# Splitting the four final loads of routed results between the queues of SyncE and ScalarE

## What is computed

```python
x = x + tanh(g_xattn[0]) * xattn(layernorm(x), ctx, ctx, mask, Wq, Wk, Wv, Wo, 16)   # 16 heads of 64
x = x + tanh(g_ffn[0]) * ffn(layernorm(x), ...)

# ffn, for h = layernorm(x), t = 1024 tokens
shared = (silu(h @ shared_gate.T) * (h @ shared_up.T)) @ shared_down.T
probs = sigmoid(h @ router_w.T + routing_bias)
scores, idx = top_k(probs, 2)                  # of 8 experts
scores = scores / scores.sum(-1)
combined = sum over the two chosen e of  w[t, e] * (silu(h @ gate_w[e]) * (h @ up_w[e])) @ down_w[e]
return shared + combined
```

## Time and profile before

| | us |
|---|---|
| executions | 178.86, 178.73, 178.04 |
| median | 178.73 |
| span of the profiled execution, first to last instruction | 177.0 |
| TensorE busy (matmul) in the span | 163.7 (93%) |
| VectorE / ScalarE / GpSimd busy | 127.1 / 109.9 / 110.7 |
| mean granted TensorE clock | 0.990 of full speed |

### The profile page before, as it was taken

The page is one execution under the profiler, slowest core; times in us unless marked ns, Lnnn a source line. Parts: engine busy times, 40 slices in busy tenths (PEclk is TensorE's granted clock), DMA queues, the critical chain, the costliest instruction groups (busy, mean ns, idle before and its releaser), DMA issues.

```text
span 177.0 us, 4529 instructions
## 1 busy us (share of the span) xinstructions
PE 163.7 (93%) x1412; PEld 139.0 (79%) x1412; DVE 127.1 (72%) x612; ACT 109.9 (62%) x404; POOL 110.7 (63%) x139
## 2 busy tenths in 40 slices
PE   7999889999999999999999999988899999998970
PEld 7777669997879998779998787986587878776860
DVE  2879988755898676888676979877857676665273
ACT  4567997558697447787646968744546666655300
POOL 3775799846786835868624768687644466656611
PEclk9999999999999999999999999999999999999996
DMA  5899995810000000000000000012222222220272
GB/s 151 280 373 378 414 403 206 352 62 0 19 2 4 15 2 4 30 21 15 30 4 0 15 21 15 17 50 54 85 76 66 74 63 67 63 77 31 57 233 90
DMA packets 11094, 17.33 MB, mean 98 GB/s; under 512 B 2075, under 2 KB 6945, under 8 KB 10944
## 3 DMA queue, kind: packets, MB, share of 16 engines
q1 hardware_dynamic: 9504, 14.59, 24.0%
q0 software_dynamic: 1280, 2.20, 3.8%
q10 hardware_dynamic: 288, 0.26, 0.4%
HBM read 9.99 MB, written 7.51 MB: 99 GB/s over the span
## 4 chain that ended last, share of the span: by engine, by line
PE 54%; DVE 12%; ACT 10%; POOL 9%; DMA 6%; issue 6%; SPq 1%; DVEq 0%; POOLq 0%
PE misc L408 8%; PE s_even L371 6%; PE o_bank L397 6%; ACT probs L722 4%; PE pt L382 4%; PE proj_q L328 4%; PE pt L658 3%; DMA ys<-probsT,xg 3%; PE proj_k L328 3%; DVE probs L931 3%; PE misc L482 3%; PE proj_q L329 2%; PE proj_q L330 2%; PE proj_k L330 2%; POOL ys L1436 2%
## 5 line engine op out<-in xcount | busy, mean ns | idle before, releaser
L722 ACT ACTIVATE probs<-probs,negmax 128x128 f32<-128x128 f32 x128 | 50.0, 394 | 8.5 <-DVE negmax L931 8.5
L1327 POOL TENSOR_TENSOR probs<-probs,rinv 128x512 f32<-128x512 f32 x32 | 33.1, 1048 | 24.4 <-DVE rinv L945 24.3
L1436 POOL DMA_INDIRECT ys<-probsT,xg x23 | 22.6, 982 | 17.1 <-issue 10.1
L722 ACT ACTIVATION_READ_ACCUMULATOR probs<-probs,negmax 128x1 f32 x128 | 24.3, 190 | 0.0
L931 DVE CUSTOM_DVE_ANT_0 probs<-s_even,mask 128x128 f32<-128x128 f32 x64 | 18.1, 283 | 3.8 <-issue 3.8
L1357 POOL DMA_INDIRECT xs<-xrow,slot x16 | 16.3, 1020 | 6.8 <-issue 3.9
L382 PE MATMUL pt<-ident_sb,probs 128*128 128x128 f32 x128 | 17.6, 277 | 1.6 <-POOL probs L1327 1.0
L371 PE MATMUL s_odd<-kT,qT 64*128 64x128 f32 x128 | 18.5, 285 | 0.0
L371 PE MATMUL s_even<-kT,qT 64*128 64x128 f32 x128 | 18.5, 284 | 0.0
L931 DVE CUSTOM_DVE_ANT_0 probs<-s_odd,mask 128x128 f32<-128x128 f32 x64 | 18.1, 283 | 0.0
L658 PEld LDWEIGHTS pt<-down_sb,v 128*128 128x128 f32 x92 | 12.1, 190 | 7.6 <-issue 7.5
(11 more groups left out here) (282 smaller groups left out, 458.8 us busy)
## 6 DMA issues: line engine op xcount, KB each, us to landing
xs<-pad SPq DMA_DIRECT2D x5, 858.0 KB, 6.3
xg<-xs SPq DMA_DIRECT2D x23, 66.0 KB, 1.9
down_sb<-down SPq DMA_DIRECT2D x1, 1152.0 KB, 9.6
probs<-ys SPq DMA_DIRECT2D x4, 256.0 KB, 4.0
gu_raw<-gu SPq DMA_DIRECT2D x3, 256.0 KB, 5.8
wk_raw<-wkT SPq DMA_DIRECT2D x2, 256.0 KB, 3.6
wq_raw<-wqT SPq DMA_DIRECT2D x2, 256.0 KB, 4.8
mask<-mask SPq DMA_DIRECT2D x8, 64.0 KB, 1.9
```

What stands on the lines that cost most here:

```text
L722: e = act.activation(probs[:, r, l, :], probs[:, r, l, :], ACT.Exp, bias=negmax[:, r, l:l + 1], scale=-1.0, accum_out=rowsum[:, r, l:l + 1])
L1327: pool.tensor_tensor(quad, quad, rinv[:, r, 4 * u:4 * u + 4].unsqueeze(2).to_broadcast([P, 4, P]), ALU.mult).then_inc(norm_done, 1)
L1436: pool.indirect_dma_start(out=ys, out_offset=bass.IndirectOffsetOnAxis(ap=xg[n % IN_FLIGHT][:, P:P + 1].bitcast(U32), axis=0), in_=y_sb[n ...
```

## The change

SyncE raises a new semaphore `y_landed` when its waits for the scatters are over, and issues loads 0 and 2 only. ScalarE waits for that semaphore after its last `block_y` and issues loads 1 and 3, ahead of `silu(2)`, `silu(3)` and its stores.

```diff
@@ semaphores
-        out_sem = sem("out_sem")
+        out_sem, y_landed = sem("out_sem"), sem("y_landed")
@@ SyncE, after `for i in range(IN_FLIGHT): sp.wait_ge(y_out[i], due[i])`
-            for n in range(4):
+            sp.sem_inc(y_landed, 1)
+            for n in (0, 2):
                 load_y(sp, n)
             store_out(sp, 0)
             store_out(sp, 2)
@@ ScalarE
             block_y(BLOCKS - 1)
+            act.wait_ge(y_landed, 1)
+            for n in (1, 3):
+                load_y(act, n)
             for unit in range(2, 4):
                 silu(unit)
             store_out(act, 1)
```

## The result

The change is slower: 179.58 us (median of 22 executions, 178.34 to 180.11) against 178.85 us for the kernel before (22 executions in the same comparison), a ratio of 1.0031 with a 95% interval of 1.0018 to 1.0045, or +0.55 us (0.3 to 0.8); the two medians lie 0.73 us apart, inside the same interval. The forecast of 178.5 us had the wrong sign, and 179.58 lies just outside the range, which ended at 179.5.

The account below looks back on a forecast made before the run. VectorE's unbroken run and the loads through GpSimd were taken as level, with GpSimd's drain ending the program. VectorE's +0.43 and an earlier GpSimd drain gave a 176.70 span (-0.27); with 1.76 added, 178.5 us, range 177.8 to 179.5.

Parts of the forecast that it names:

- the landings: Loads 2 and 3 on two queues: taken to land at 170.9 and 171.2, bounds 1.0 us earlier and unchanged.
- 1 us of slack: Load 0 at VectorE's first addition: landed at 169.3, over 1 us before it was wanted at 170.39.
- The room I saw: DMA engines between 168.5 and 169.0: only 115 GB/s moved while the second issue's packets were late, against 377 later.
- The rival "nothing": Both queues feed the same engines and loads 2 and 3 land as before: 178.7 us, chance 0.20.
- ScalarE's wait and issues: ScalarE before silu(2): wait costs 0.13 us, two issues put silu(2) at 167.17, covered by its 0.78 us idle.
- the long value: A load issue of 1.06 us falling to ScalarE: silu(2) starts at 167.80, VectorE's run begins 0.19 us late.
- GpSimd's drain: End of program: drain counts from GpSimd's last addition, 3.36 us after it, so it would end at 175.96.
- The port: SBUF: VectorE's two-input additions and GpSimd's pair additions exclude each other, costing VectorE 0.43 us in the kernel before.
- My +0.43: VectorE's run: two delays of 0.43 from earlier pair additions, less the present 0.43; bounds -0.43 and +1.0.
- The sum: Whole program: SyncE's drain last, span 176.70 against 177.0, or -0.27 us, giving 178.5 us.
- 0.76: Chance given to a time that can't be told from no change, within 0.5% or 0.89 us.
- my slower case: ScalarE held by its issues past 167.8, so silu(3), hidden(3) and add_shared(0) start late: middle 179.4 us, chance 0.20.

Follow-up runs that it names:

- wait_only: The kernel before, with SyncE raising y_landed and ScalarE waiting for it, all four loads still issued by SyncE: ratio 1.0002 (0.9966 to 1.0038).
- pool_pad: The kernel before, with one more GpSimd addition (128x128, result unused) behind its two pair additions: ratio 1.0020 (0.9998 to 1.0041).
- no_pool: The kernel before, with both pair additions moved from GpSimd to VectorE: ratio 0.9985 (0.9968 to 1.0003).
- change_again: The change itself, measured once more against the kernel before: ratio 1.0015 (0.9990 to 1.0041).
- halves: The change, with SyncE issuing loads 0 and 1 and ScalarE loads 2 and 3: ratio 1.0028 (1.0003 to 1.0053) to the kernel before.
- no_tail: The kernel before, without GpSimd's scatters of blocks 21 and 22, which hold no row for these inputs: ratio 1.0010 (0.9988 to 1.0031).
- hold: The change, with all four loads back on SyncE and ScalarE issuing two tiny loads (1 KB in all) instead: ratio 1.0031 (1.0008 to 1.0053) to the kernel before.
- hold_again: All four loads on SyncE, two tiny loads issued by ScalarE, measured a second time against the kernel before: ratio 1.0024 (1.0000 to 1.0048).
- after_pool_one: The change, with GpSimd's second pair addition moved to VectorE: ratio 0.9995 (0.9977 to 1.0013) to the kernel before.
- act_late: The change, with ScalarE issuing loads 1 and 3 after silu(2) and silu(3): ratio 1.0023 (1.0000 to 1.0046) to the kernel before.
- hold_act: All four loads on SyncE; ScalarE waits for y_landed, then makes five 128x64 copies in place of its two issues: ratio 1.0005 (0.9979 to 1.0032) to the kernel before.

## Why the prediction was wrong

**The step that failed** is that of the landings: "With the durations of before they would land at 170.6 and 170.8 ... Bounds: 1.0 us earlier, and unchanged." I carried times to landing measured with one queue over to two, and gave no bound on the late side. For load 0 I wrote "That instruction also delays load 0 by 0.07, against 1 us of slack: nothing", and counted only the issue. Measured: load 0 took 4.85 us instead of 3.09, 0.7 more than its slack; load 2 landed at 6.08 instead of 5.42. The room I saw, the dip to 115 GB/s, was there and was filled (0.50 MB in the first 3.0 us instead of 0.35), but it did not move the last landing: load 3 came at 6.25, before at 6.07. What was moved earlier was of two loads at once, so neither was complete earlier, and the rate then fell to 238 GB/s where it had been 314 and more.

**The rival "nothing"** came nearest, and I cited it for the wrong thing. The section of the Trainium skill's page DMA: Bandwidth & Descriptors on issuing engines that are not separate queues says that the transfers run on the same engines and interleave. By that rule the trace agrees, 0.25 and 0.25 MB in the first 3.0 us, and landings at 4.85 and 5.04 us. I took from it only that a gain may fail to come. The same trace shows more: SyncE's queue moved 0.10 MB less than before in that time, and load 0 was late by it.

**ScalarE's wait and issues.** The wait cost nothing that shows, as said (wait_only 1.0002, 0.9966 to 1.0038, the end at 10.66). The issues took 1.49 us, since the long value that I had set aside was the one that came. For it I had expected VectorE's run 0.19 us late; it started at 3.37 as before.

**GpSimd's drain.** Right: 3.36 us after GpSimd's last addition in 15 of the 18 profiles, and it follows GpSimd (pool_pad, no_pool). It was the step at which I had to choose, and the choice held. But it worked against me: I had the additions end 0.8 us earlier, and they ended 0.60 later, which is the whole of the 0.60 us by which the end moved (11.33 against 10.73).

**The port.** Right in kind. In the change, one of the first four additions met a pair addition (the four took 2.21 us instead of 1.72), the last two then 0.76 instead of 1.19: it moved, and cost nothing more. In change_again it did not even move. My +0.43 rested on early pair additions and fell with them. One reading in it was inexact: 0.852 is not 0.424 plus the rest of GpSimd's addition, of which 0.57 us were left by its recorded times (0.99 in all). Its length is that of an addition that began 0.14 us before the other's recorded end; the same working gives 0.15 in the change, 0.14 and 0.15 in halves. halves, in which GpSimd did start early (170.81), shows the exclusion twice among the four additions (the longest took 0.83):

```profile
L1281 DVE TENSOR_TENSOR x_sb<-probs,x_sb x6: 418/426/831, 170.6 to 174.4; 128x256 f32<-128x256 f32 x6
```

Even there the first of the two cost nothing, since the third addition, at 5.88 us, was waiting for load 1, landed at 5.79.

**The sum.** -0.27 forecast, +0.60 in the profiles, +0.55 in the runs (+0.27 in change_again, not clear of nothing). That the size stayed under the 0.5% to which I had given 0.76 was luck: I expected a small gain there, and it was a small loss by a path I had not priced. The middle of my slower case, 178.9 to 180.2, is 179.55, not 179.4, which changes nothing here. The signs of "slower" were there with 0.20, but by another mechanism (ScalarE held), which the change had mostly covered.

## What to carry to other kernels

A second queue is no second set of engines: feeding both at once made the loads at their heads land together here, 0.2 us apart in five profiles, near the time at which one queue had landed its second. Where a consumer wants loads in an order, keep them in that order on one queue, and ask of a load's slack whether it survives sharing. And at the end of a program look at each engine's drain, not only at the last store: here taking one addition off GpSimd gained 0.38%, while no way of moving the loads gained anything clear of noise.

## What the runs showed that I had not expected

GpSimd's drain ends 3.36 us after its last addition, in fifteen profiles; 3.34 in pool_pad, 3.20 in no_tail, and 4.81 after a scatter (no_pool). SyncE's takes 0.007 and ScalarE's 0.15 us.

The second issue of a queue that is fed at this moment takes 0.77 to 1.36 us, on SyncE or on ScalarE, against 0.43 to 0.46 for later ones. When both queues are fed at once with two loads each or more, both second issues end within 6 ns of each other (in the change, change_again, halves, hold, hold_again and after_pool_one; in the change: 166.27 + 1.08 on ScalarE, 166.30 + 1.06 on SyncE), and this also happens when ScalarE's is a transfer of 1 KB (hold: 0.98). In act_late, where ScalarE issued 1.5 us later, its two issues took 0.83 together. It belongs to the moment and not to the queue or the size. Without the last scatters it was 0.83 (no_tail), with them 0.85 in pool_pad and 0.77 in hold_act, so they are not shown to be it either. Its cause was not found.
